# Experts in a gathered graph layer: node groups of 2, 4, 4, ... tiles, 30 tiles of all experts computed during the gather instead of 28, and the next event's entry read in the middle of an event

## The reference, cut to what matters

```python
def reference(x, src, dst, edge_weight, W, b, Wr, br, W1, b1, W2, b2, gamma, beta):
    h = layernorm(x)
    x = x + segment_sum((h @ W)[src] * edge_weight[:, None], dst, 12500) + b
    y = layernorm(x)                                     # one sequence of 12,500 rows
    p = softmax(mean(y, axis=0) @ Wr + br)               # 8 experts, one choice for all rows
    p = softmax(p * capacity_scale(p))
    top_w, top_i = top_k(p, 2); top_w = softmax(top_w)
    e = gelu(y @ W1[i] + b1[i]) @ W2[i] + b2[i]          # 256 -> 512 -> 256, for the two chosen i
    return x + layernorm(sum(top_w * e) + y) * gamma + beta
```

## Time and profile before

| | |
|---|---|
| median of 3 runs | 2414.32 us (2414.03 to 2417.64) |
| the profiled execution's own time | 2414.97 us |
| its span | 2413.0 us, mean granted clock 0.984 |
| TensorE busy | 2200.5 us, 91% of the span |
| GpSimd busy | 1617.3 us, 67% |
| ScalarE, VectorE busy | 1167.4 us (48%), 1028.8 us (43%) |
| DMA | 414.72 MB, 171 GB/s over the span |

### The profile page before, as it was taken

The page is one execution under the profiler, slowest core; times in us unless marked ns, Lnnn a source line. Parts: engine busy times, 40 slices in busy tenths (PEclk is TensorE's granted clock), DMA queues, the critical chain, the costliest instruction groups (busy, mean ns, idle before and its releaser), DMA issues. The chain is left out here.

```text
span 2413.0 us, 40876 instructions
## 1 busy us (share of the span) xinstructions
PE 2200.5 (91%) x9817; PEld 1693.0 (70%) x9818; DVE 1028.8 (43%) x2967; ACT 1167.4 (48%) x3163; POOL 1617.3 (67%) x1627
## 2 busy tenths in 40 slices
PE   2488999999999989999999999899999989999998
PEld 1367667776667766666676777676766768998897
DVE  7884232322223222232322322232321246888896
ACT  3577666656456545344434333232232117554663
POOL 6777777777777777777777777777777752333432
PEclk9999999999999999999999999999999999999999
DMA  9855565658555655555556655555555543233321
GB/s 373 328 167 163 159 181 163 190 164 272 173 182 171 188 175 177 177 180 164 168 173 180 192 170 189 165 178 181 178 173 175 182 143 107 88 106 131 114 82 54
DMA packets 218864, 414.72 MB, mean 172 GB/s; under 512 B 36227, under 2 KB 130230, under 8 KB 218728
## 3 DMA queue, kind: packets, MB, share of 16 engines
q0 software_dynamic: 75008, 204.90, 28.5%
q1 hardware_dynamic: 143288, 206.10, 26.1%
q10 hardware_dynamic: 432, 2.40, 0.3%
HBM read 332.61 MB, written 80.65 MB: 171 GB/s over the span
## 5 line engine op out<-in xcount | busy, mean ns | idle before, releaser
L533 POOL DMA_INDIRECT G<-xr_d,SRC x1467 | 1394.6, 951 | 447.3 <-issue 297.9
L1025 DVE TENSOR_SCALAR OH<-CST,DL,WR 128x128 f32<-128x128 f32 x1564 | 566.9, 369 | 1275.5 <-PE ps L1339 928.6
L1339 PE MATMUL ps<-G,OH 128*128 x3128 | 743.3, 391 | 109.4 <-DVE OH L1025 81.6
L1339 PEld LDWEIGHTS ps<-G,OH 128*128 128x128 f32 x3128 | 592.7, 194 | 269.4 <-issue 193.4
L1329 PE MATMUL ps<-W2u,H 128*128 128x256 f32 x1792 | 407.0, 386 | 22.3 <-issue 21.3
L1329 PEld LDWEIGHTS ps<-W2u,H 128*128 128x128 f32 x1792 | 340.5, 192 | 87.9 <-issue 42.7
L1318 PE MATMUL ps<-YU,W1u 128*128 128x512 f32 x896 | 394.0, 592 | 1.5 <-issue 1.1
L1318 PEld LDWEIGHTS ps<-YU,W1u 128*128 128x128 f32 x896 | 170.1, 190 | 192.6 <-issue 183.7
L733 ACT ACTIVATE YE<-ps 128x512 f32<-128x512 f32 x112 | 66.8, 596 | 474.8 <-PE ps L1329 474.8
L726 ACT ACTIVATE H<-ps,b1a 128x512 f32<-128x512 f32 x224 | 153.8, 687 | 208.0 <-PE ps L1318 207.7
L612 ACT ACTIVATE OHX<-OHT,WR 128x128 f32<-128x128 f32 x194 | 67.4, 394 | 225.9 <-PE ps L1339 225.9
(11 more groups left out here) (206 smaller groups left out, 2342.2 us busy)
## 6 DMA issues: line engine op xcount, KB each, us to landing
W1u<-in_W SPq DMA_DIRECT2D x56, 512.0 KB
W2u<-in_W SPq DMA_DIRECT2D x56, 512.0 KB
y_d<-YE SPq DMA_DIRECT2D x56, 512.0 KB, 5.4
G<-xr_d,SRC POOLq DMA_INDIRECT x1467, 2.9
x_d<-X SPq DMA_DIRECT2D x98, 128.0 KB
yt_d<-YT SPq DMA_DIRECT2D x98, 128.0 KB, 2.3
XR<-in_x SPq DMA_DIRECT2D x97, 128.0 KB, 2.9
XS<-in_x SPq DMA_DIRECT2D x24, 512.0 KB, 19.2
```

Source lines behind the costliest of these rows:

```text
L533: e.indirect_dma_start(out=G[0:rows(s), s % RING, :], out_offset=None, in_=x if s < FRESH else xr_d, in_offset=bass.IndirectOffsetOnAxis(a ...
L1025: e.tensor_scalar(OH[:, s % OHR, :], iota, DL[:, s:s + 1], WR[:, s + 1:s + 2], ALU.is_equal, ALU.mult).then_inc(s_oh, 1)
L1339: e.matmul(ps[:, 0, 0:D], OH[:, r, :], Gf[:, bass.ds(g + r * D, D)], start=False, stop=True, skip_group_check=True).then_inc(s_main, 1)
```

## The change

The groups become 2, 4, 4, ... tiles (still 25). AHEAD becomes 8, so 2 + 7 * 4 = 30 tiles get all 8 experts during the gather, in 64 units, the first 8 of them of half size. 17 groups of 4 tiles are left behind it. Units are handed out from tile 14 on, and a half unit counts half. The first unit lands in tile 15; tiles 89 to 96 get 17 unit events instead of 15 (tile 96 four instead of three), and tile 97 has seven as before. `unit_up`, `unit_down`, `unit`, `unit_out` and the transfers take the size of the group; on TensorE a register decides between two copies of the code. The register load of the next event's entry moves from the head of an event to behind `chores` in a section and between `unit_down` and `unit_up` in a unit. `pre_of` now gives post groups 1, 2, 4, 6, 8, 9, 11 and 13. The staging of x keeps its groups of 4 under the names XG and xtiles.

```diff
 GT = 4
-NG = (NT + GT - 1) // GT
-AHEAD = 7
+XG = (NT + GT - 1) // GT
+SMALL = 2
+NG = (NT - SMALL + GT - 1) // GT + 1
+AHEAD = 8
...
+def group(t):
+    return 0 if t < SMALL else (t - SMALL) // GT + 1
+
+
 def tiles(g):
-    return range(g * GT, min((g + 1) * GT, NT))
+    a = SMALL + (g - 1) * GT
+    return range(a, min(a + GT, NT)) if g else range(SMALL)
...
-    room = [max(0.0, 0.75 * slots[t] - 3.5) * most[t] if t >= 18 else 0.0 for t in range(NT)]
+    room = [max(0.0, 0.75 * slots[t] - 3.5) * most[t] if t >= 14 else 0.0 for t in range(NT)]
+    size = [len(tiles(k // E)) / GT for k in range(UNITS)] + [1.0]
     free, u, out = 0.0, 0, []
     for t in range(NT):
-        free += room[t] * (UNITS + 1) / sum(room)
-        n = max(0, min(int(free + 0.5), UNITS + 1 - u)) if t < NT - 1 else UNITS + 1 - u
-        free -= n
+        free += room[t] * sum(size) / sum(room)
+        n = 0
+        while u + n <= UNITS and (free >= size[u + n] / 2 or t == NT - 1):
+            free -= size[u + n]
+            n += 1
...
-                e.dma_start(YU[:, :, :], yt_d[g, :, :, :]).then_inc(yu_in, 16)
+                w = len(tiles(g)) * P
+                e.dma_start(YU[:, :, 0:w], yt_d[g, :, :, 0:w]).then_inc(yu_in, 16)
...
-                e.wait_ge(s_fin, 4 * n + m)
-                top = NT - g * GT - m
+                e.wait_ge(s_fin, first_of[n] + m)
+                top = NT - tiles(g)[0] - m
...
             def unit(u):
+                w = len(tiles(u // E)) * P
...
-                    e.activation(H[:, i, :], ps[:, UP[i % 2], :], ACT.Gelu, bias=b1a[:, u % E, i:i + 1]).then_inc(s_gelu, 1)
+                    e.activation(H[:, i, 0:w], ps[:, UP[i % 2], 0:w], ACT.Gelu, bias=b1a[:, u % E, i:i + 1]).then_inc(s_gelu, 1)
...
-            def unit_up(u):
+            def unit_up(u, m):
...
-                        ins = e.matmul(ps[:, UP[i % 2], :], W1u[:, c, i * P:(i + 1) * P], YU[:, c, :], start=(c == 0), stop=(c == 1))
+                        ins = e.matmul(ps[:, UP[i % 2], 0:m * P], W1u[:, c, i * P:(i + 1) * P], YU[:, c, 0:m * P], start=(c == 0), stop=(c == 1))
...
-            def unit_down(u):
+            def unit_down(u, m):
...
-                    for h in range(2):
-                        j = 3 - (2 * p + h)
+                    for h in range(m // 2):
+                        j = m - 1 - (m // 2 * p + h)
...
+            def by_size(do):
+                u = e.snap(u_r, min_val=0, max_val=UNITS - 1)
+                with e.If(u < E):
+                    do(u, SMALL)
+                with e.Else():
+                    do(u, GT)
...
+            def following():
+                at = e.snap(ev_r, min_val=0, max_val=NEV - 2)
+                e.load([due, kind], EVT[0:1, bass.ds(at * 2 + 2, 2)])
+                e.reg_add(ev_r, ev_r, 1)
+
             def event(a, r, g):
                 with e.While(lambda: e.snap(rel) <= r):
-                    at = e.snap(ev_r, min_val=0, max_val=NEV - 2)
-                    now = e.snap(kind)
-                    e.load([due, kind], EVT[0:1, bass.ds(at * 2 + 2, 2)])
-                    e.reg_add(ev_r, ev_r, 1)
+                    e.reg_mov(now_r, e.snap(kind))
+                    now = e.snap(now_r)
                     with e.If(now < UPS):
                         v = e.snap(v_r, min_val=0, max_val=FINAL - 1)
                         chores(v)
+                        following()
                         with e.If(now == END):
                             begin(v, g + (r - 1) * D)
                         e.reg_add(v_r, v_r, 1)
                     with e.Else():
                         with e.If(now > UPS):
-                            unit_down(e.snap(u_r, min_val=0, max_val=UNITS - 1))
+                            by_size(unit_down)
                             e.reg_add(u_r, u_r, 1)
+                        following()
                         with e.If(now < DOWNS):
-                            unit_up(e.snap(u_r, min_val=0, max_val=UNITS - 1))
+                            by_size(unit_up)
```

More of the change, by code:

```diff
@@ L28, with xtiles, part, place_in @@
 END, EXTRA, UPS, BOTH, DOWNS = range(5)
+def xtiles(g):
+    return range(g * GT, min((g + 1) * GT, NT))
+def group(t):
+    return 0 if t < SMALL else (t - SMALL) // GT + 1
 def tiles(g):
-    return range(g * GT, min((g + 1) * GT, NT))
+    a = SMALL + (g - 1) * GT
+    return range(a, min(a + GT, NT)) if g else range(SMALL)
+def part(t):
+    return slice((t - SMALL) % GT, (t - SMALL) % GT + 1)
+def place_in(t):
+    return t - tiles(group(t))[0]
 def slot(t):
-    return len(tiles(t // GT)) - 1 - t % GT
+    return len(tiles(group(t))) - 1 - place_in(t)
 def roots():
@@ L249, in gnn_ffn @@
         place = {g: n for n, g in enumerate(order)}
+        first_of = [sum(len(tiles(g)) for g in order[:n]) for n in range(NG)]
         s_route, s_rpe, s_ract = sem("dve_route"), sem("pe_route"), sem("act_route")
@@ L268, in gnn_ffn @@
         SUMS, IDX, GATES = 7, (15, 22), 31
-        between = [1 if 6 <= g < 12 else 3 if g == XBUF else 2 if g == XBUF + LOTS[0] else 1 if g > XBUF else 0 for g in range(NG)]
+        between = [1 if 6 <= g < 12 else 3 if g == XBUF else 2 if g == XBUF + LOTS[0] else 1 if g > XBUF else 0 for g in range(XG)]
         EARLY = sum(between)
@@ L406, in _ @@
             store_x(1)
-            for g in range(XBUF, NG):
+            for g in range(XBUF, XG):
                 load_x(g)
@@ L429, in _ @@
                     keep_rows(n)
-                    if n == post[0] * GT + 4 * GT:
+                    if n == tiles(post[0])[0] + 4 * GT:
                         for t in tiles(post[0]):
@@ L742, in scale_x @@
                 for g in lots[b]:
-                    for j, t in enumerate(tiles(g)):
+                    for j, t in enumerate(xtiles(g)):
                         r_ = LAST if t == NT - 1 else P
@@ L1042, in fresh @@
                 newton_steps(n - 1, (4 * j + 2, 4 * j + 3))
-            for g in range(6, NG):
+            for g in range(6, XG):
                 x_stats(g)
@@ L1331, in unit_down @@
                     ins.then_inc(s_dn, 1)
-            v_r, u_r, ev_r, due, kind, rel = (e.alloc_register(n) for n in ("section", "unit", "event", "due", "kind", "ahead"))
+            def by_size(do):
[4 more added lines that the diff above has]
+                    do(u, GT)
+            v_r, u_r, ev_r, due, kind, now_r, rel = (e.alloc_register(n) for n in ("section", "unit", "event", "due", "kind", "now", "ahead"))
             for r_ in (v_r, u_r, ev_r):
@@ L1444, in down @@
                     n = place[post[k - 2]]
-                    e.wait_ge(s_z, 4 * n + len(tiles(post[k - 2])))
+                    e.wait_ge(s_z, first_of[n] + len(tiles(post[k - 2])))
                 if k == 0 and i == 0:
```

59 lines of the change are left out of this document (31 added, 28 removed).

## The result

The changed kernel takes **2428.92 us** (median of 6 runs, 2425.64 to 2431.56) against 2414.89 us (6 runs, 2413.54 to 2417.64) for the kernel before beside it: **1.0057** times as long, 95% interval 1.0044 to 1.0070. The prediction was 2408.5 us, with 0.36 for faster and a range of 2403 to 2432 us. So the time lies in the range, on the side that was not forecast. What happened is the outcome of rival 1: TensorE becomes the gather's bound.

A forecast was written before the change was run, and what follows sets the result against it. GpSimd's issuing was taken to bound the gather and TensorE what follows; 7.9 us less behind the gather, 1 more for stops and 0.5 for the start, gave 6.4 less: 2408.5 us, range 2403 to 2432.

The forecast's parts named there:

- rival 1: Gather: TensorE becomes the bound, over 50 us late at slot 1510; 2411 to 2420 us (0.20) or more (0.26).
- The part in the gather: Slots 130 to 1510: TensorE's 1732 us balance GpSimd's 1733, so the added unit work costs nothing.
- Units, 852 us: Gather, TensorE: 8 half and 56 full units at 14.2 us each, 852 us, where it was 795.
- Sections, 273 us: Gather, TensorE: 88 sections at 3.1 us on the mean, 273 us.
- Slots, 607 us at 0.44: Gather, TensorE: 1380 slots at 0.44 us each, 607 us.
- The start: TensorE at slot 130, where the balance begins: some 37 us late.
- GpSimd's start, +0.5 us: First loop pass: a fourth code fetch could delay GpSimd and the gather by up to 5.4 us; 0.5 taken.
- Rival 4: Gather loop no longer stays in TensorE's code memory: 195 passes with a stop, 1050 us more; chance 0.02.
- The removal: Behind the gather: the group of 2 tiles goes, 11.5 us less on TensorE.
- The stops: Post groups: waits for YL reaching TensorE, 1 us more; ends 4 us less and 5 us more.
- The end of the program: Behind the last product: the last group has 4 tiles, 3.6 us more for sums, norms and store.
- rival 3: Two groups in a row stop TensorE at post group 9, or a fourth fetch delays GpSimd: 5 us each; 0.06.

The follow-up runs named there:

- units_at_roots_pairs_3: Changed kernel with units planned into tiles at ScalarE's roots and groups done ahead beside post groups 1, 2, 4, 6, 8, 10, 12, 14; third run: 2411.75 us, 1.0000.
- one_unit_earlier_2: The kernel of units_at_roots_pairs_3 with every unit from tile 48 on planned one unit earlier, second run: 2411.79 us, 0.9994 times the kernel before.
- read_at_head: Changed kernel with the register load of the next event back at the head of each event: 2472.18 us, 1.0257; with the long gather 1.0099.
- pairs_apart: Changed kernel with groups done ahead finished beside post groups 1, 2, 4, 6, 8, 10, 12, 14: 1.0067, again 1.0036, both with the long gather.
- changed_again: Changed kernel, unedited, in a batch with the long gather: 3246.11 us against 3228.55 for the kernel before, 1.0052.

## Why the prediction was wrong

**The step that failed** is the balance in "The part in the gather", TensorE's sum of 1732 us from slot 130 to slot 1510, and with it the sentence that the 57 us of added unit work are paid from idle time. The sum came to 1756.5 us, and GpSimd took 1734.1. By its terms (which depend by 2 to 3 us on where one part is cut off from the next):

- *Units, 852 us*: 848.8 us. Right, by two errors that the runs took apart: I gave the moved load nothing, and with the load back at the head units take 899.0 us; and I took the stop of before, 0.55 us, as what would be there without the move, where it is 0.9 (49.7 us in 57).
- *Sections, 273 us*: 272.5 us.
- *Slots, 607 us at 0.44*: 635.0 us. **This is the term of the sum that was mis-sized.** A slot at full clock takes 0.432 us, which would be 596 us. But 42 slots took 0.85 us, in the stretches at 0.50, most of them behind the stops at the roots: 17.6 us. The rest, 21 us, are small stops at the turns of the loop and behind the sections. I had priced a long section from its start to its end, and the clock comes down behind it.
- *The start*: 40.5 us late at slot 130, where I had 37.

So TensorE was 62.8 us late at slot 1510 instead of 37, where up to 50 costs nothing. The last slots gave back 0.82 us each, as I had it, and 19.9 us were left at the last one against the 4.9 of before: the 15 us of the table.

The error could have been seen before the run. For the kernel before, the same terms give 607 + 273 + 795 = 1675 us, so TensorE would have been idle for 58 of GpSimd's 1733 us. Its trace has 24.8 us of waits for one-hots, and slots took 624 us beside them. The idle time that was to pay for 57 us of units was less than half of that. This is also what makes the difference between the two kernels: TensorE's time from slot 130 to slot 1510 grew by 26 us, with units up by 32 to 34, sections by 6, other time in slots by 5, and waits for one-hots down by 19. The stretches at 0.50, 55 us before and 61 after, are hardly a part of that difference; they are a part of the level that my sum missed. Taking most of them away with the stops at the roots is one way to win the time back, as units_at_roots_pairs_3 shows, where TensorE waits for one-hots in the middle again; less unit work is another.

**GpSimd's start, +0.5 us.** Its last issue came 6.8 us later. The fourth fetch, which I named and priced at up to 5.4 us, came: gaps of 3.2 and 4.9 us (start to start, 1.25 being normal) at issues 67 and 69, 5.6 us more than a plain pace. I took 0.5 because I saw GpSimd 57 slots ahead; but being ahead is what fills the ring and stops it. The low value was chosen against my own row. It did not matter for this result, by luck: TensorE is as far at slot 124 as before, and it, not GpSimd, sets the end. With TensorE in time it would matter, as in one_unit_earlier_2, where GpSimd's last issue at 1979.8 us sets the last slot.

**Rival 1** had the right outcome and mark (over 50 us late at slot 1510, no wait up to slot 1564), but was to come from longer sections, 3.3 to 3.5 us each. These stayed at 3.2; the slots between them took more than I had. Its other sign, the ring stopping GpSimd from 1700 us on, is not in this trace, only in read_at_head's.

**Rival 4** did not come: the four pieces stay through the loop. The Trainium skill, page "Runtime: NRT & Kernel Launch", section "Instruction fetch mechanics", ties a taken branch out of a window of two 16 KB pages to a fetch; here the trace disagrees, with 4 fetches on q8 up to 110 us and the other 23 of the 27 after 1990 us.

**Behind the gather.** The removal was priced rightly: from 394.6 to 389.2 us for the post groups; stops in them grew by 6.6 us, so 12.0 us of work less against 11.5. The stops were priced at 1 with 5 as an end; two late `YL` in a row cost 7.4 us in one group, above that end. pairs_apart brings 4 of it back. The end of the program costs 0.9 us, not 3.6. This is rival 3, of which both halves came, on top of rival 1; I had them as alternatives.

So the expected gain was there: 12 us of work left the path. It was given back in the gather, where TensorE was 26 us later at slot 1510 than before (62.8 against 36.8) with room for 13. Its units took only 32 us more than the 816.8 of before, though 57 us of them were added, for the moved load paid the rest; without that the change would have lost some 45 us more. By the runs the tiles at the roots without units and the crowded pairs together are worth 14 us, of which the pairs have 4.

**Still open.** Why GpSimd's pace differs between executions (1728.3 to 1734.1 us for the same 1380 slots), which is as much as the last differences. What the fourth fetch would give back was not tried by itself, nor the branch on the size, nor units at the roots alone without the long gather.

## What to carry to other kernels

When work is moved into the shadow of another engine, the room there is not the idle share but the lateness at the point where the shadow ends. Draw up the balance term by term, and first for the kernel before: it must give the waits that its trace shows, here 24.8 us and not 58. Work put right behind another engine's longest chain fills a stop, and the same work two tiles on doesn't: where in the order it lies was worth about 10 us here, beside the 12 that were removed. And a load in an instruction stream belongs behind a stock of long instructions, where it cost 4.4 us over all units; at the head of the body it was 0.8 us each time. That only pays where the engine is the bound: in the kernel before the same move gave 0.1%.

## What was not expected of the hardware

A stop of TensorE of about 2 us is often followed by a stretch at half clock, in which a slot takes 0.85 instead of 0.432 us: 12 of the 15 stretches of the changed kernel begin within 6 us of a stop of 1.6 us or more. With 42 slots in them they cost 17.6 us beside 35 us of stops for XH and AS. It is not certain: in units_at_roots_pairs_3 five stops of 2.0 to 3.1 us have no such stretch behind them.

In some batches the gather of the same program takes 800 us longer, with the same 0.95 us for GpSimd's instruction and the same 23.01 us for a post group. Their traces show TensorE standing still for 2 to 15 us about a hundred times (107 in changed_again), in 40 of them with no releaser named. The first place is early, where VectorE waits for a product that ended at 31.1 us:

```profile
29.93 1.21 PE L1301 MATMUL ps<-ones_b,cmpb 128*98 128x1 bf16 x13
...
51.22 0.25 DVE L972 CAST FROW<-ps 1x98 int32<-1x98 f32 x1 [20.93 <-remote]
```

In the first profile of the changed kernel the same VectorE instruction starts at 31.0 us. GpSimd was issuing indirect DMAs in both cases; what delays the signal is not settled, nor is why one chip showed both. There the version with units at the roots has 1.0105 and the changed kernel 1.0052, but in different batches, and one and the same kernel (without the code for unsorted edges) had 1.0085 and 1.0037 in two of them. So whether that order is worse there is not shown.
